# Expert 0's first 128 rows computed token-stationary during the last routing, with residual, projections and order redone

## The reference

```
x = x + tanh(g0) * attn0(layernorm(x), ctx)      # 16 heads of 16, q and k normalised per head
x = x + tanh(g1) * tanh(layernorm(x) @ W @ A1 @ A2 + bias)
x = x + tanh(g2) * attn1(layernorm(x), ctx)      # 8 heads of 64, keys: tokens and context (487)
x = x + tanh(g3) * moe(layernorm(x))

def moe(h):                                      # 896 tokens, 8 experts, each token goes to 2
    w, idx = top_k(softmax(h @ gate_w.T), 2); w = w / w.sum()
    out = sum over experts e of ce[:, e] * ((silu(h @ gup_e[:1024].T) * (h @ gup_e[1024:].T)) @ down_e.T)
```

## Time and profile before

| | before |
|---|---|
| median of three runs | 582.26 us |
| the profiled execution | 582.92 us |
| its span, first to last instruction | 581.1 us |
| PE busy | 554.3 us, 95% |
| VectorE busy | 396.3 us, 68% |
| ScalarE busy | 320.4 us, 55% |
| GpSimd busy | 272.8 us, 47% |
| mean granted TensorE clock | 0.995 |

### The profile page before, as it was taken

The page is one execution under the profiler, slowest core; times in us unless marked ns, Lnnn a source line. Parts: engine busy times, 40 slices in busy tenths (PEclk is TensorE's granted clock), DMA queues, the critical chain, the costliest instruction groups (busy, mean ns, idle before and its releaser), DMA issues.

```text
span 581.1 us, 13542 instructions
## 1 busy us (share of the span) xinstructions
PE 554.3 (95%) x5542; PEld 476.5 (82%) x5542; DVE 396.3 (68%) x759; ACT 320.4 (55%) x632; POOL 272.8 (47%) x237
## 2 busy tenths in 40 slices
PE   8999999999989999999999999998899999989994
PEld 8776667677657878888888898877899999979994
DVE  7877568578696666767666766756577677746752
ACT  3554555555674665566555556654466656736631
POOL 3755755765740164657566555731203234421424
PEclk9999999999999999999999999999999999999998
DMA  7910840000000000000000000019364557716111
GB/s 252 361 49 2 321 191 3 1 3 2 2 2 1 2 1 2 8 8 18 18 9 18 9 26 9 17 36 412 83 252 157 176 199 253 262 28 237 29 21 24
DMA packets 24090, 50.92 MB, mean 88 GB/s; under 512 B 7072, under 2 KB 17104, under 8 KB 20688
## 3 DMA queue, kind: packets, MB, share of 16 engines
q1 hardware_dynamic: 18560, 45.20, 21.5%
q0 software_dynamic: 4224, 3.70, 3.5%
q10 hardware_dynamic: 1232, 1.01, 0.6%
HBM read 37.89 MB, written 13.31 MB: 88 GB/s over the span
## 4 chain that ended last, share of the span: by engine, by line
PE 81%; DVE 6%; ACT 5%; POOL 4%; issue 3%; DMA 1%; POOLq 0%; DVEq 0%; ACTq 0%
PE ps L59 15%; PE ps L60 14%; PE ps L61 14%; PE ps L609 5%; PE ps L627 4%; PE ps L752 4%; PE ps L770 4%; PE ps L740 4%; ACT P L1623 3%; DVE KN L1142 3%; PE ps L643 3%; PE ps L517 2%; POOL P L1929 2%; PE ps L818 2%; PE ps L524 2%
## 5 line engine op out<-in xcount | busy, mean ns | idle before, releaser
L1929 POOL TENSOR_SCALAR P<-P,rinv 112x487 f32<-112x487 f32 x56 | 87.4, 1576 | 49.7 <-DVE rinv L1185 49.4
L1142 DVE TENSOR_REDUCE KN<-ps 112x4 f32<-112x1500 f32 x32 | 55.0, 1718 | 28.7 <-PE ps L609 28.6
L59 PE MATMUL ps<-XGf,WH 128*128 128x256 f32 x252 | 71.3, 283 | 0.0
L60 PE MATMUL ps<-XGf,WH 128*128 128x256 f32 x252 | 71.3, 283 | 0.0
L426 POOL DMA_INDIRECT out<-WS,rows_i x16 | 28.7, 1792 | 90.8 <-ACT WS L1770 87.2
L61 PE MATMUL ps<-XGf,WL 128*128 128x256 f32 x252 | 71.3, 283 | 0.0
L1867 POOL TENSOR_TENSOR sr<-sv,mhalf 125x32 f32<-125x32 f32 x13 | 70.7, 5436 | 1.1
L1502 DVE TENSOR_TENSOR WL<-WR,WH 128x1024 fp32r<-128x1024 f32 x48 | 57.1, 1218 | 14.2 <-ACT WH L1824 10.0
L1623 ACT ACTIVATE P<-ps 125x1344 f32<-125x1344 f32 x32 | 41.4, 1293 | 32.8 <-PE ps L627 32.7
L1686 ACT ACTIVATE P<-ps,nm 112x487 f32<-112x487 f32 x64 | 42.0, 665 | 29.2 <-DVE nm L1177 29.2
L1824 ACT ACTIVATE WH<-WR 128x1024 fp32r<-128x1024 f32 x48 | 48.7, 1049 | 0.1
(11 more groups left out here) (282 smaller groups left out, 1531.1 us busy)
## 6 DMA issues: line engine op xcount, KB each, us to landing
WR<-in_gupT SPq DMA_DIRECT2D x16, 1024.0 KB, 5.1
WR<-in_dwnT SPq DMA_DIRECT2D x8, 1024.0 KB, 10.2
xs<-ZT SPq DMA_DIRECT2D x14, 516.0 KB, 6.0
CT<-in_ctxT SPq DMA_DIRECT2D x1, 2250.0 KB, 12.3
P<-xs SPq DMA_DIRECT2D x7, 256.0 KB, 10.7
P<-xs SPq DMA_DIRECT2D x9, 128.0 KB, 2.6
Wk<-in_L_xattn_Wk SPq DMA_DIRECT2D x2, 512.0 KB, 11.2
Wv<-in_L_xattn_Wv SPq DMA_DIRECT2D x2, 512.0 KB, 11.0
```

Of the source, the lines that this page charges most:

```text
L59: e.matmul(out, ah, bh, start=start, stop=False)
L60: e.matmul(out, ah, bl, start=False, stop=False)
L1142: e.tensor_reduce(heads(KN[b % 2][0:NQ, 3, :])[:, 4 * k:4 * k + 4, 16], ps[0:NQ, 0:4, 0:NC], AX.X, ALU.max, negate=True).then_inc(s("smax" ...
L1929: e.tensor_scalar(P[:, k, 0:487], P[:, k, 0:487], rinv[:, k:k + 1], None, ALU.mult).then_inc(s("psc"), 1)
```

## The change

*Early tile.* Expert 0's first 128 rows are filled by batches 0 to 5: before batch 6 takes its positions, `pad` raises expert 0's next free place to at least 128. SP loads these rows (XGe) when the scatters of six batches have landed, and the parts `ear` compute them as one token-stationary tile (24 matmuls of 512 columns for gate and up, eight transposes, 24 of 256 for down) between the steps of the last routing. Expert 0's weights are loaded earlier, into a place that is free earlier (the WR and WH buffers change places in SBUF), and their low halves are made by GpSimd (`low`).

*Second tile.* Rows 128 to 255 of expert 0 are the parts `second`, again token-stationary, after the last scatter. Experts 1 to 7 run as before; expert 1's six splits now stand ahead of `second`. The weight of the early tile is applied by ScalarE at the start of its expert list, behind a wait for all of EX.

*Last pair.* The last V goes to a bank of its own, so that three of the four groups of the last output projection (`woa`) run ahead of it.

*Residual.* The gated biases are made once (`tgb`), GpSimd adds them to X early (`xb`), and the residual is one VectorE instruction that reads PSUM.

*Projections.* The output projection of layer one and, from batch 3 on, the query projection use `matmul3`, with splits `wd`, `xtl` and `aTl`.

*Loads.* The five weights of layer two and the gate weights share a semaphore; WO is loaded after layer one's last output projection.

*Order.* All tables have new times. WARM has 98 transposes instead of 176: 62 + 10 before the first expert and 18 + 26 in the last routing go, 30 + 8 before the second tile come.

The core of the diff:

```diff
+EARLY_FROM = 6
+
+EARLY = ((-4.15, 'pad'), (8.86, 'ear', 'x'), (9.06, 'ear', 'xh'), (10.14, 'ear', 'xl'), (11.12, 'ear', 'u', 0),
...
-WARM = {("kp", 0, 1, 0): 36, ("spk", 0, 2): 24, ("xt", NB - 1, 3): 18, ("rt4", NB - 1): 26, ("xin", 0): 62,
-        ("up", 0, 0): 10}
+WARM = {("kp", 0, 1, 0): 36, ("spk", 0, 2): 24, ("second", "x"): 30,
+        ("second", "u", 0): 8}
...
+    put("load", 1, 0)
+    put("load", 1, 1)
+    put("load", 1, 2)
+    put("second", "load")
+    put("pair", 1)
     put("ahead", 0)
-    put("pair", 1)
     for c in range(3):
         put("load", 2, c)
-    put("xin", 0)
-    units = [(x, dc) for x in range(NE) for dc in range(4)]
+    for c in range(6):
+        put("split", 1, c)
+    put("second", "x")
+    put("xin", 1)
+    put("pair", 2)
+    for q in range(4):
+        put("second", "u", q)
+    units = [(x, dc) for x in range(1, NE) for dc in range(4)]
...
+        def tensor_token(e, w, which, part, q=0):
...
+            elif part == "u":
+                z_, part_ = divmod(q, 2)
+                w.wait_ge(dve, d_ + 1)
...
+                for z in range(2):
+                    o = z * 2048 + part_ * 1024 + z_ * 512
+                    w.wait_ge(*split_done(0, o // 1024))
+                    t = matmul3(e, ps[:, up_banks[q], :], [XGTo[:, v, z * 128:(z + 1) * 128] for v in range(2)],
+                                [W[:, o:o + 512] for W in (WH[0], WL[0])], z == 0, z == 1)
+                t.then_inc(pe, 1)
...
+            elif part == "d":
+                for c in range(8):
+                    w.wait_ge(dve, d_ + 4 + c // 4)
+                    w.wait_ge(*split_done(0, 4 + c // 4))
+                    t = matmul3(e, ps[:, out_bank, 0:256], [HTo[v][:, c * 128:(c + 1) * 128] for v in range(2)],
+                                [W_[:, 4096 + c * 256:4352 + c * 256] for W_ in (WH[0], WL[0])], c == 0, c == 7)
...
             e.activation(ve[:, 0:1], mhalf[0:NQ, 0:1], ACT.Silu)
-            w.wait_ge(s("scatter"), 32 * NB)
-            e.dma_start(XG[:, 1, :], xs[128:256, 0:D]).then_inc(s("xg_first"), 16)
+            w.wait_ge(s("wts"), 16 * NE)
+            w.wait_ge(s("ea_pe"), 8)
+            e.activation(YS[:, 0, :], ps[:, 2, 0:256], ACT.Copy, scale=weight(0, 0)).then_inc(s("yc0"), 1)
...
+                elif stage == "pad":
+                    for sem_, v in emptied(("rt4", EARLY_FROM - 1)):
+                        w.wait_ge(sem_, v)
+                    e.tensor_scalar(base_[:, EARLY_FROM % 2, 0:1], base_[:, EARLY_FROM % 2, 0:1], 128.0, None,
+                                    ALU.max).then_inc(s("pad"), 1)
...
-                    e.tensor_tensor(tt[:, b % 2, :], ps[0:NQ, bank(*src), 0:256], bias[:, bi, :],
-                                    ALU.add).then_inc(bank_sem(*src), 1)
-                    if r != 2:
...
+                        e.scalar_tensor_tensor(X[:, b, :], ps[0:NQ, bank(*src), 0:256], tg[0:NQ, r // 2:r // 2 + 1],
+                                               X[:, b, :], ALU.mult, ALU.add).then_inc(bank_sem(*src), 1)
...
+                elif stage == "xb":
+                    b, r = i
+                    w.wait_ge(s("once"), 1)
+                    w.wait_ge(s("norm"), o_("norm", b, r - 1))
+                    e.tensor_tensor(X[:, b, :], X[:, b, :], bias[:, r - 1, :], ALU.add).then_inc(s("xb"), 1)
```

More of the change, by code:

```diff
@@ L109 @@
[L109 to L113, removed]
@@ L219, in attention_order @@
         at(pair_at[NPAIR - 4] + d, stage, 0, c)
+    for d, stage, *i in EARLY:
+        at(pair_at[NPAIR - 1] + d, stage, *i)
     for _, _, entry in sorted(timed):
@@ L230, in expert_order, with done @@
     put = order.put
-    for x in range(2):
-        for c in range(3):
-            put("load", x, c)
-    put("pair", 0)
+    def done(p):
+        put("rows", p)
+        if p == NE - 1:
+            put("oversent", p)
+        put("sent", p)
+        put("over", p)
+        if p < NE - 1:
+            put("oversent", p)
+        if p + 1 < NE:
+            put("ahead", p + 1)
+        if p + 3 < NE:
+            for c in range(3):
+                put("load", p + 3, c)
+    put("load", 1, 0)
[3 more added lines that the diff above has]
+    put("pair", 1)
     put("ahead", 0)
-    put("pair", 1)
     for c in range(3):
         put("load", 2, c)
-    put("xin", 0)
-    units = [(x, dc) for x in range(NE) for dc in range(4)]
+    for c in range(6):
[6 more added lines that the diff above has]
+    units = [(x, dc) for x in range(1, NE) for dc in range(4)]
     for i in range(len(units) + 2):
@@ L252, in expert_order @@
             put("hid", *units[i - 1])
+        if i == 1:
+            put("second", "d")
+            done(0)
         if i >= 2:
@@ L256, in expert_order @@
             if pdc == 3:
-                put("rows", p)
-                if p == NE - 1:
-                    put("oversent", p)
-                put("sent", p)
-                put("over", p)
-                if p < NE - 1:
-                    put("oversent", p)
-                if p + 1 < NE:
-                    put("ahead", p + 1)
-                if p + 3 < NE:
-                    for c in range(3):
-                        put("load", p + 3, c)
+                done(p)
         if i < len(units) and dc >= 1 and x + 1 < NE:
@@ L812, in tensor_attention @@
                         w.wait_ge(s("ws"), 6)
-                    for g in range(nt):
+                    for g in range(3 if (stage, n) == ("wo", LAST_A) else 0, 3 if stage == "woa" else nt):
                         if NB <= n < LAST_A:
@@ L1631, in scalar_attention @@
                                  ACT.Copy).then_inc(bank_sem(src), 1)
+                elif stage == "wd":
+                    k, = i
+                    if k:
+                        w.wait_ge(s("dve0"), Q_SET)
+                    else:
+                        w.wait_ge(s("in_b"), BIAS_SET)
+                    high, W = ((Wps[0], Wp), (Wqs[0], Wq0))[k]
+                    e.activation(high, W, ACT.Copy).then_inc(s("wda"), 1)
                 elif stage == "k1c":
@@ L1930, in pool_attention @@
                                         ALU.mult).then_inc(s("psc"), 1)
+                elif stage == "low":
+                    split_low(e, w, *i)
                 elif stage == "rt5":
```

578 lines of the change are left out of this document (395 added, 183 removed), and 14 rows, old and new, of tables (EARLY, FIRST).

## The result

The changed kernel takes 590.42 us (median of 4 runs, 589.93 to 590.7) against 582.72 for the one before on the same chip: ratio 1.0128, 95% interval 1.0116 to 1.0140. It is 7.7 us slower; 581.3 was forecast, with 587.5 as the upper end. The profiled execution took 590.4 us (span 588.7) against 582.92 (span 581.1), 7.5 more.

A forecast was written before the change was run, and what follows sets the result against it. It took PE, busy 95% of 581.1 us, and the nearly idle hand-over as what bounds the kernel. Terms -4.8 - 1.0 - 0.3 + 3.3 + 1.8 = -1.0 gave 581.3 us, range 576.0 to 587.5.

The forecast's parts named there:

- The hand-over: Last output projection to expert products: 8.4 us less work, but start 11.7 later behind EX loads and queued splits; net +3.3.
- the batches 21.4 us apart: Sign in the first attention: batches were to follow each other at 21.3 us instead of 22.1.
- ScalarE's wait: Sign at the hand-over: ScalarE without work for some 7 us until the eighth EX load, then seven instructions in a row.
- the idle PE ahead of the second tile: Sign at the hand-over: PE without work for about 8 us, then the second tile's first matmuls at wider spacing.
- The early tile's gate and up products: Sign in the last routing: the early tile's up matmuls between about 397 and 408, at unchanged full clock.
- First attention, -4.8: Layer one's attention: cheaper projections and new order save 0.8 us per batch over six batches' worth; ends -1.8 and -6.6.
- Second attention, -1.0: Layer two's attention: nearly the same order and matmuls, VectorE loses 0.4 us per residual; ends 0 and -3.
- The last routing, -0.3: Routing before the experts: GpSimd's five low halves and three table loads against work saved; ends -2 and +2.8.
- T: The moment when the last scatter has landed and SP goes on, 415.35 us before the change.
- rival D: Batch 7's routing gets late through ScalarE's table loads and the low halves: T moves +2.8, 584.1 us; chance 0.12.
- the clock, +1.8: Second tile's start: PE idles some 8 us and restarts at a lower clock, costing 1.8 us; ends 0 and +4.
- Rival C: Slower: ScalarE's queue behind the EX loads, between T and the second tile, decides; +5.1 net, 585.6 us; chance 0.23.

The follow-up runs named there:

- f3: The changed kernel with layer one's output projections and the five split query projections as single plain fp32 products of the high parts: 593.68 us.
- e3: The changed kernel with GpSimd's gain of batch 1's queries again behind its power for batch 1's keys, as before the change: 589.18 us.
- g1: Changed kernel plus edits of f1, e2 and e3, with expert 0's low halves divided: GpSimd makes 0 to 2, VectorE 3 to 5: 572.52 us, ratio 0.9811.
- e1: The changed kernel with ScalarE's eviction of the early tile behind expert 1's six high splits instead of ahead: 582.06 us, ratio 0.9977 to the kernel before.
- g3: The changed kernel with 14 warm-up transposes on PE ahead of batch 6's transposes: 589.97 us.
- e2: The changed kernel with GpSimd making the fifth low half of expert 0 behind the last routing's scatters: 588.12 us.
- f1: Changed kernel, hand-over reordered: early tile's eviction waits only for its own EX load, four expert 1 splits behind second tile's input, 30 warm-ups gone: 578.49 us.
- e4: The changed kernel with each low half of expert 0 made by four GpSimd instructions of 256 columns instead of one of 1024: 591.97 us.
- g2: g1 with 13 warm-up transposes on PE, 8 ahead of batch 7's prefix sum and 5 ahead of the early tile's first hidden transposes: 572.85 us.

## Why the prediction was wrong

The span was to shrink by 1.0 us and grew by 7.6. The step that failed is the price of giving GpSimd more work in layer two. The prediction asked only whether GpSimd's own queue would be late; it had no term for VectorE being held by it, and that cost 3.1 us (1.2 in the second attention, 1.9 in the last routing). Three more terms were wrong: GpSimd's swapped order in the opening, 1.65 us, had none; the savings by order in both attentions were 1.6 and 1.8 us too large; and the full clock in the early tile was assumed, 1.5 us. The hand-over, the largest price, was nearly right. Of the signs that were named, the batches 21.4 us apart, ScalarE's wait (8.7 us) and the idle PE ahead of the second tile (9.0 us) came. The early tile's gate and up products came late, from 404.39 to 414.5 instead of 397 to 408, at a clock of 0.57 from 404 to 408. And the first attention was not 3 us shorter, which had been named as a sign of being wrong.

**First attention, -4.8: measured -1.9.** The loop did what was forecast: 21.38 us from batch to batch (21.3 was said), and its two parts hold (f3: 0.23 a batch for cheaper projections, the rest order). But from the sixth S0 to the thirtieth it gained 3.2 and not 4.8. Five batches gained 3.9, the 0.8 each that was said; the sixth lost 0.7, since before the change it took only 20.96 us and not 22.1 (21.64 after). And the opening lost 1.65, which had no term at all. I had read the order at the places where projections moved, and not at the opening, where one swap on GpSimd put 5.46 us behind a wait of 6.82 (shown by e3).

**Second attention, -1.0: measured +2.0.** Up to 357 us the lead stays between 1.8 and 2.3 us, so the same matmuls in nearly the same order gained nothing; from there to the last V it is lost. PE's visible waits there are 0.66 us for a VectorE instruction behind ScalarE's first splits of expert 0, and 1.30 for the copy that GpSimd held. In g1, without the hold, the last V comes 194.0 us behind the first scores, 195.2 after and 193.2 before: the hold is worth 1.2. The other 0.8, and the 1.0 that was to be gained, are left to the order; no run here takes that part further.

**The last routing, -0.3: measured +2.3.** Here the failed step stands in one place of the prediction: five low halves were priced on GpSimd's own queue, "ahead of batch 7's rstd", with some 1.2 us. That price was zero: each took 2.33 to 2.39 us, and the fifth ended at 402.12, 3.6 us before GpSimd began batch 7's rstd (405.74), for which it waited for VectorE. What they cost was VectorE's time: from last V to T the changed kernel took 20.33 us; e1 and g3, whose clock was full up to batch 7's transposes, 18.8; e2, all but without the hold as well, 16.9 (397.59 to 416.38, 397.54 to 416.37, 398.84 to 415.78). So 1.9 us were the hold and 1.5 the clock, which had been booked at "unchanged full clock" for the early tile. Without both the routing is 1.1 faster than the 18.07 of before: better than the forecast -0.3, which held the 1.2 us for a late low half. The three table loads cost 1.28 each and nothing around them, and rival D's price was not paid.

That GpSimd and VectorE share an access to SBUF stands in the Trainium skill (SBUF — State Buffer, SBUF: two separate sides): an exclusive lock, taken for a whole instruction, and it asks two SBUF inputs or a two-port mode of VectorE. The trace agrees: the instructions held are a copy and a tensor_scalar within SBUF, while a copy from PSUM at 397.49 took its 0.62 us beside the same low halves; and a subtraction of two SBUF inputs of 8 columns beside the sixth (L1640, 417.17) took 1.36 instead of 0.16. Not every instruction within SBUF was held: beside the same work a reciprocal of 8 columns (393.46) took its 0.19 us and a tensor_scalar of one column (392.30) 0.14. It is the rule that spoke against this change, and the prediction weighed another one in its place, the throughput of GpSimd: 2.4 us a low half, which the trace bears out with 2.33 to 2.39 and which decided nothing.

**The hand-over, +3.3, and the clock, +1.8: measured +5.7 for both.** Start at T + 16.4 (T + 15.8 was said), 12.3 more than before. From there to PE's last product 146.9 us instead of 153.5, 6.6 less, where -8.4 of work and +1.8 of clock had been said. The 1.8 can be seen: the first nine products of the second tile follow each other at 0.43 us instead of 0.23. The 8.4 is then what is left, not measured by itself. e1 and f1 show that it was the queue on ScalarE and VectorE that held the start: it came at T + 9.3 and T + 5.9. Rival C named this mechanism and its side, and lacked the losses ahead of T; rival D put T at +2.8 (measured +2.4), for another reason.

The sum by measured terms: -1.9 + 2.0 + 2.3 + 5.7, less 0.5 for a shorter tail of scatters, is +7.6 of span. The chances were split by sign of the known terms; that two terms could both turn, because one cause outside the sum (a hold between engines) acts on every stage where GpSimd was given work, was in none of the cases.

## What to carry to other kernels

Work given to an idle GpSimd is not free where VectorE copies, casts or normalises within SBUF at the same time: list those VectorE instructions beside each new GpSimd instruction that reads SBUF (here all were subtractions of two SBUF inputs), and look whether one of them is on the chain. Where such work must be moved there, put it where VectorE reads PSUM or stands idle, and not two in a row ahead of such an instruction (e2, g1); cutting them smaller without a gap did not help (e4). And ahead of anything that waits for loads in an in-order queue, place what is ready: here one instruction moved let the second tile start 7.1 us earlier.

## What was not expected of the hardware

- VectorE's SBUF copy (0.43 us alone) took 2.27 (after) and 3.12 (e4) beside GpSimd's two-input subtractions, its tensor_scalar (0.41 alone) 2.79 and 2.17. The hold went on over the boundary between two GpSimd instructions (after) and over two boundaries and more (e4).
- GpSimd's subtraction of 128x1024 took 2.33 to 2.39 us, four of 128x256 in a row 2.8.
- The granted clock fell to the lower level (1.2 GHz instead of 2.4) for a few us between 397 and 418 in ten of the twelve traces of the changed kernel and its variants, at places that differ, and not in e1 and g2. Runs of one kernel differ in this too: e1's ten have mean clocks of 0.993 or 0.994 and of 0.987 to 0.989, and where the second group's fell no trace shows. A fall ahead of batch 7's transposes went with 1.5 us more from the last V to T, one behind them with none.
